# Expert rows packed in units of 64: 20 expert tiles a pass with four two-expert tiles, where there were 23 single-expert tiles

## The reference, cut to what matters

```python
B, T, D = 16, 512, 256
FF, E, TOPK = 1024, 8, 2
# for each of 1024 tokens, 2 experts are given (expert_indices, expert_weights)
hidden = gelu(layernorm(x_token) @ w1[e])      # 256 -> 1024
y      = hidden @ w2[e]                        # 1024 -> 256
x_out  = x_token + sum over its two experts of weight * y + bias
```

## Time and profile before

| | |
|---|---|
| median of three runs | 1342.62 us (1338.91 to 1346.79) |
| the profiled execution | 1340.46 us, its span 1338.7 us |
| TensorE busy | 1232.7 us, 92% of the span |
| VectorE / ScalarE / GpSimd busy | 67% / 54% / 45% |
| mean granted TensorE clock | 0.972 of 2.4 GHz |
| moved by DMA | 168.17 MB, 126 GB/s on average |

### The profile page before, as it was taken

How to read it: one execution, slowest core, us unless ns; L and a number is a source line. 1 busy time by engine, 2 the same in 40 slices (tenths; PEclk the granted TensorE clock), 3 DMA queues, 4 the chain that set the end, 5 groups by cost and what they waited for, 6 DMA issues and landing times. The chain is left out here.

```text
span 1338.7 us, 17191 instructions
## 1 busy us (share of the span) xinstructions
PE 1232.7 (92%) x6044; PEld 998.6 (75%) x6044; DVE 896.1 (67%) x1483; ACT 724.6 (54%) x1124; POOL 599.4 (45%) x534
## 2 busy tenths in 40 slices
PE   4699989999999999999988889899999999999982
PEld 2387677887878878888766658778778788888871
DVE  7998846557666665676878967578666665645354
ACT  3355443664735537356556657467666463553632
POOL 5335554346351442525747627367434522224014
PEclk9799999999999999999989979899999999999996
DMA  7001343647365472563230023665446644554554
GB/s 213 16 25 40 86 124 105 187 124 207 102 185 149 125 205 92 149 191 118 68 94 16 17 64 119 157 164 140 128 115 163 172 146 139 179 154 131 123 162 130
DMA packets 107333, 168.17 MB, mean 126 GB/s; under 512 B 10024, under 2 KB 85296, under 8 KB 107248
## 3 DMA queue, kind: packets, MB, share of 16 engines
q1 hardware_dynamic: 88016, 120.39, 28.1%
q0 software_dynamic: 12608, 40.65, 15.3%
q10 hardware_dynamic: 6624, 6.03, 1.3%
HBM read 134.79 MB, written 17.06 MB: 113 GB/s over the span
## 5 line engine op out<-in xcount | busy, mean ns | idle before, releaser
L1930 PE MATMUL psum<-fwv,hid 128*128 128x256 f32 x1024 | 239.6, 383 | 0.0
L576 POOL TENSOR_TENSOR rstd<-varis,half_neg 128x4 f32<-128x4 f32 x64 | 93.8, 1465 | 309.6 <-DVE varis L2721 145.4
L1930 PEld LDWEIGHTS psum<-fwv,hid 128*128 128x128 f32 x1024 | 193.6, 193 | 27.0 <-issue 1.0
L1971 PEld LDWEIGHTS psum<-xst,ew 128*128 128x128 f32 x1472 | 178.6, 193 | 17.1 <-issue 6.5
L1971 PE MATMUL psum<-xst,ew 128*128 128x128 f32 x1472 | 181.0, 276 | 5.6 <-ACT xst L1092 3.2
L1979 PE MATMUL psum<-ew,hidt 128*128 128x256 f32 x736 | 166.9, 380 | 2.7 <-ACT hidt L1098 2.7
L1979 PEld LDWEIGHTS psum<-ew,hidt 128*128 128x128 f32 x736 | 138.8, 190 | 24.8 <-ACT hidt L1098 3.5
L580 POOL TENSOR_SCALAR xhat<-rows_ring,negmean,rstd 128x256 f32<-128x256 f32 x108 | 110.9, 1039 | 18.7 <-PE psum L1840 12.3
L1098 ACT ACTIVATE hidt<-psum 128x512 f32<-128x512 f32 x92 | 54.9, 597 | 108.3 <-PE psum L1971 108.2
L1005 ACT ACTIVATE hid<-psum 128x512 f32<-128x512 f32 x128 | 74.7, 596 | 64.6 <-PE psum L1851 44.2
L693 POOL DMA_INDIRECT xs<-xf_rows,token_of_slot x46 | 56.3, 1224 | 88.5 <-PE psum L1959 74.2
(11 more groups left out here) (277 smaller groups left out, 2465.6 us busy)
## 6 DMA issues: line engine op xcount, KB each, us to landing
ew<-in_w SPq DMA_DIRECT2D x92, 1024.0 KB, 5.7
rows_ring<-bias_rows POOLq DMA_DIRECT2D x28, 512.0 KB, 5.6
rows_ring<-in_x SPq DMA_DIRECT2D x14, 512.0 KB, 4.6
rows_ring<-y POOLq DMA_DIRECT2D x14, 512.0 KB, 6.4
out<-rows_ring SPq DMA_DIRECT2D x14, 512.0 KB, 5.0
rows_ring<-space POOLq DMA_DIRECT2D x12, 512.0 KB, 4.7
ys_rows<-ys ACTq DMA_DIRECT2D x46, 128.0 KB, 4.8
xf_rows<-ew SPq DMA_DIRECT2D x2, 1024.0 KB, 4.6
```

Source lines behind the costliest of these rows:

```text
L576: pool.tensor_tensor(dst, src, half_neg[:, 0:src.shape[1]], ALU.pow).then_inc(done, 1)
L1930: last = nc.tensor.matmul(rows4[:, k, :], hid[:, j % NHID, k * P:(k + 1) * P], fwv[:, j, :], start=j == 0 and k % 2 == 0, stop=j == FC - 1 ...
L1971: last = nc.tensor.matmul(bank_e[:, j * P:(j + 1) * P], ew1[:, c, at:at + P], xst[:, c, :], start=c == 0, stop=c == DC - 1)
```

## The change

The rows of an expert are now counted in units of 64. A pass needs at most 2048/64 + 8 - 1 = 39 units, so 20 tiles (NT) of two units do. 16 of them are plain: both units are of one expert. Four, the mixed tiles, hold two units that may be of different experts (the odd unit that an expert has left over). The table of experts has 24 entries a pass, 16 for the plain tiles and 2 for each mixed one. The places "d" of turns 5 to 7, "x" of turns 14 and 15 and "d" of turn 16 are gone, so there are 40 tiles in all, and eight of them are mixed: those at "a" of turns 5, 6, 7, 8, 14 and 15, "d" of turn 11 (run at the start of turn 12) and "b" of turn 13.

A mixed tile turns its first product around: the 64 token columns of a unit are the weights and 512 columns of that unit's w1 move, so tokens come out on the partitions, unit 0 on partitions 0 to 63 and unit 1 on 64 to 127 (`two_up`). In the built program these matmuls have an array tile of 128x64 at column 0 or 64, where all of a plain tile's have 128x128. ScalarE copies the 128x512 result to `hid_rows` (`rows_of_two`), TensorE transposes it (`two_turn`), and the gelu follows as before. The second product has 64 columns of `hidt` as weights, once for each unit (`two_down`). A mixed tile needs two experts' w1 and w2, 4 MB through the same 2 MB buffer: the front half of the buffer takes the first halves of both w1, the back half the second halves, and each is overwritten by half of both w2 after `two_up(n, 0)` and `two_up(n, 1)`.

```diff
+UNIT = P // 2
+UNITS = NASG // UNIT + E - 1
+NT = (UNITS + 1) // 2
...
+MIXED_AT = ((5, "a"), (6, "a"), (7, "a"), (8, "a"), (11, "d"), (13, "b"), (14, "a"), (15, "a"))
...
             def load_expert(n):
...
-                e = sp.value_load(table[0:1, n % NT:n % NT + 1], min_val=0, max_val=E - 1)
-                if n:
+                experts = uses(n) if n in MIXED else [expert_in(tile_of(n))]
+                if n - 1 in MIXED:
+                    sp.wait_ge(half_down.sem, half_down.count(MIXED.index(n - 1), "h"))
+                elif n:
                     await_step(sp, up, n - 1, "b")
+                if n in MIXED:
+                    for x, e in enumerate(experts):
+                        load_w1(two_w1[0][:, x], e, slice(0, FF // 2))
+                else:
+                    load_w1(ew1, experts[0], slice(0, FF))
...
+            def load_mixed_w2(n):
+                experts = uses(n)
+                for half_no in range(2):
+                    await_step(sp, up, n, "ab"[half_no])
+                    for x, e in enumerate(experts):
+                        load_w2(two_w2[half_no][:, x], e, half_no * FC // 2, FC // 2)
...
+            def rows_of_two(n, half_no):
+                await_step(act, up, n, "ab"[half_no])
+                nc.scalar.activation(hid_rows[:], bank_e, ACT.Copy).then_inc(rows_up.sem, 1)
...
+            def two_up(n, half_no):
+                if half_no == 0:
+                    pe.wait_ge(xst_ready, n + 1)
+                else:
+                    await_step(pe, gelu, n, "a")
+                pe.wait_ge(slot_loaded[half_no], landed(n, 1))
+                for c in range(DC):
+                    for x in range(2):
+                        last = nc.tensor.matmul(bank_e[unit_rows(x), :], xst[:, c, unit_rows(x)], two_w1[half_no][:, x, c, :],
+                                                start=c == 0, stop=c == DC - 1)
+                last.then_inc(up.sem, 1)
+
+            def two_turn(n, half_no):
+                await_step(pe, rows_up, MIXED.index(n), "ab"[half_no])
+                for j in range(4):
+                    last = nc.tensor.transpose(bank_e[:, j * P:(j + 1) * P], hid_rows[:, j * P:(j + 1) * P], ident[:])
+                last.then_inc(turned.sem, 1)
+
+            def two_down(n):
+                await_step(pe, gelu, n, "b")
+                for half_no in range(2):
+                    pe.wait_ge(slot_loaded[half_no], landed(n, 2))
+                    for j in range(4 * half_no, 4 * half_no + 4):
+                        for x in range(2):
+                            last = nc.tensor.matmul(bank_e[unit_rows(x), 0:D], hidt[:, j, unit_rows(x)],
+                                                    two_w2[half_no][:, x, j % 4, :], start=j == 0, stop=j == FC - 1)
+                    if half_no == 0:
+                        last.then_inc(half_down.sem, 1)
+                last.then_inc(tiles_done, 1)
```

More of the change, by code:

```diff
@@ L72 @@
 TURN_OF = {n: i for (i, _), n in TILE_AT.items()}
+MIXED = [TILE_AT[at] for at in MIXED_AT]
+assert sum(n < NT for n in MIXED) == NMIX and len(MIXED) == 2 * NMIX
 NORM_TURN = [3, 10]
@@ L96, in await_step, with tile_of, landed @@
     eng.wait_ge(steps.sem, steps.count(min(run, steps.runs - 1), name))
+def tile_of(n):
+    before = sum(n - n % NT <= m < n for m in MIXED)
+    return PLAIN + before if n in MIXED else n % NT - before
+def landed(n, part):
+    return 16 * (n + 3 * sum(m < n for m in MIXED) + (2 * part if n in MIXED else 1))
 def numbered(name, n):
@@ L364, in hybrid_kernel @@
         last_pow = steps("last_pow", ["ln", "p"], 1)
-        route = steps("route", ["idx", "expert", "one", "rank", "n", "nf", "ni", "start", "end", "pos", "past", "tab",
-                                "slot"], 1)
+        route = steps("route", ["idx", "expert", "one", "rank", "n", "u", "p", "uf", "two", "left", "upto", "shift", "from", "at",
+                                "ends", "moved", "row", "pos", "past", "past2", "second", "late", "tab", "slot"], 1)
         route_pe = steps("route_pe", ["spread", "counts", "ends", "slots", "experts"], 1)
@@ L2186, in turn @@
                 p = only_rec(i)
-                a, b, c, d = (TILE_AT[i, place] for place in "abcd")
+                a, b, c = (TILE_AT[i, place] for place in "abc")
                 tile_in(a)
                 value_columns(i)
-                tile_up(a, 0)
+                two_up(a, 0)
                 recept_columns(i)
-                tile_up(a, 1)
+                two_turn(a, 0)
                 freed(ev2, i - 1, "e1")
@@ L2195, in turn @@
                 transposes_rec(p)
+                two_up(a, 1)
                 channel_key(i - 1, 0)
+                two_turn(a, 1)
                 channel_key(i - 1, 1)
-                tile_down(a)
                 freed(ev3, p, "c1")
                 receptances(i - 1)
+                two_down(a)
                 channel_key(i - 1, 2)
@@ L2408, in turn_12 @@
                 channel_key(11, 0)
-                tile_in(25)
+                tile_in(22)
                 channel_key(11, 1)
-                tile_up(25, 0)
+                two_up(22, 0)
                 channel_key(11, 2)
-                tile_up(25, 1)
+                two_turn(22, 0)
                 channel_key(11, 3)
+                two_up(22, 1)
                 freed(ev2, 11, "e1")
@@ L2562, in turn_15 @@
             def turn_15():
-                tile_in(37)
+                tile_in(33)
                 value_columns(15)
-                tile_up(37, 0)
+                two_up(33, 0)
                 channel_key(14, 0)
-                tile_up(37, 1)
+                two_turn(33, 0)
                 recept_columns(15)
+                two_up(33, 1)
                 channel_key(14, 1)
-                tile_down(37)
+                two_turn(33, 1)
                 freed(ev2, 14, "e1")
@@ L2573, in turn_15 @@
                 transposes_rec(13)
-                tile_in(38)
+                two_down(33)
                 channel_key(14, 2)
-                tile_up(38, 0)
                 channel_key(14, 3)
-                tile_up(38, 1)
                 channel_value(14, 0)
-                tile_down(38)
                 freed(ev3, 13, "c1")
```

571 lines of the change are left out of this document (307 added, 264 removed).

## The result

The changed kernel takes 1368.41 us in the median of four runs (1367.65 to 1370.07); the kernel before takes 1340.76 us beside it (1338.11 to 1346.79). The ratio is 1.0201, with a 95% interval of 1.0163 to 1.024: 27 us slower, where 13.5 us faster was forecast. The profiled execution has a span of 1366.0 us, against 1338.7.

A forecast was written before the change was run, and what follows sets the result against it. TensorE, busy 92% of the span, was taken as the bound. Terms -43.4 - 1.7 + 14.6 + 2.5 + 5.1 + 4.6 + 4.8 gave -13.5 us: 1329.1 us, 1.0% faster, range 1318 to 1375.

The forecast's parts named there:

- The side-by-side work: Mixed tiles on TensorE: two array halves overlap, half a `two_up` in 5 steps, `two_down` in 17; eight tiles 14.6 us dearer.
- The six tiles: Six tiles fewer on TensorE at 7.24 us each take out 43.4 us.
- The changes of the array's tile: Mixed tiles switch between 128x128 and 128x64, 48 changes at 0.05 us each, 2.5 us; bounds 0 and 0.14 a change.
- Rivals 1 and 2: Mixed tiles: columns take turns, 1371 us, chance 0.22; weight loads not hidden under the other column's matmul, 1351 us, chance 0.12.
- The middle norm: Turns 5 to 7: `rec_products` waits 1.7 us each for `norm_mid` to empty the transposes' banks, 5.1 us.
- The wait at the end (about 13 us): TensorE idles about 13 us before the last `rec_products`; of the last tile's 7.24 us, 4.8 are lost.
- Waits of 1.7, 1.7 and 1.2: 4.6 us: `two_down` waits for w2 in turns 14, 15 and 8, landing 6.2 us after issue; nothing in turns 5 to 7, 12, 13.
- the prediction's own sign of being wrong: Waits before the mixed tiles' steps adding up to more than 15 us would show the forecast wrong.
- Rival 3: Traffic of 4 MB around each mixed tile makes w2 or next w1 land late (11.8 us); 1346 us, chance 0.06.
- Nothing was put for the clock: The sum held no term for time lost to TensorE's half clock; forecast 0.
- "I put nothing" for ScalarE: ScalarE's 16 copies of 0.60 us for 12 gelus and 12 short copies fewer cost nothing, as it has room (54%).
- the removed tiles as pure gain: Removed tiles counted as -43.4 us of TensorE time, and -1.7 us of waits at the next turn's `tile_in`.

The follow-up runs named there:

- plain_40: The changed kernel with its eight mixed tiles run as plain tiles of one expert, the second expert's rows multiplied by wrong matrices; ratio 0.9904 to the kernel before.
- no_w2: The changed kernel without loading the mixed tiles' second matrices, their second product using what the first matrices left in the buffer; ratio 1.0003 to the kernel before.
- quiet: The changed kernel with POOL's two adds of the bias into rows_ring issued behind the gather for the next tile; ratio 1.0051 to the kernel before.
- fill_half: The changed kernel with 8, 8, 14 and 5 scratch matmuls ahead of the mixed tiles' second product in turns 6, 7, 14, 15; ratio 1.0162 to the kernel before.
- early_acts: The changed kernel with a relu earlier in turn 8, and conv_in and its transposes one step earlier in turn 12; ratio 1.0111 to the kernel before.
- x_outer: The changed kernel with all left-half matmuls issued before the right half's in both products of a mixed tile; ratio 1.0214 to the kernel before.

## Why the prediction was wrong

- **The side-by-side work: right that it happens, and the sum by luck near.** -26.3 us forecast, -28.8 measured, but no term was right by itself. The six tiles gave 41.4 us of work (plain_40), not 43.4. The mixed tiles cost 12.6, not 14.6 + 2.5 = 17.1, and this by two errors against each other. The overlap is better than forecast: both halves of the array start together, so half a `two_up` is four steps and not five, and `two_down` 16 and not 17; no right record waits for the second left one. The changes of the array's tile are dearer: about 0.3 us for a change and back, 0.15 a change, where 0.05 was taken and 0.14 was the upper bound: some 7 us instead of 2.5. The steps alone cost 6 us (2 x 1.72 + 3.46 + 0.87 for 7.02, eight times), and 6 + 7 is about the 12.6 that was measured.
- **What the rivals said of the array.** Rivals 1 and 2 are refuted, although the time fell within 3 us of rival 1's 1371: a total that fits a rival is no evidence for it, the group of L2055 is. The Trainium skill's rule that different column groups run concurrently ("TensorE: Matmul & The Clock Gate", Part 3) holds here, with 6.9/3.61 = 1.9x for two column tiles. Its rule of the same part that weights load beside matmuls only where the row group differs does not hold for this kernel's f32 records (the same part also names the background weight buffer, and the rows go with that). A drain when the tiling mode changes ("TensorEngine Tiling (Array Packing)", Key Properties, in the Trainium skill) would show as a cost like these 0.3 us; that it is a drain isn't shown, since nothing here changes the tile without changing the weights' columns too.
- **The middle norm: right** in its cause, with 3 x 1.54 = 4.6 us for 5.1. **The wait at the end (about 13 us): right**, 13.03, and the merges take 7.41 us unbroken as forecast (7.4). What was missed there is a second wait on the same chain, 5.25 us ahead of the gate products of p = 15, of which before shows 0.5.
- **"Waits of 1.7, 1.7 and 1.2: 4.6 us": the step that failed.** 16.3 us were measured: 3.9 in turn 6, 3.8 in turn 7, 6.4 in turn 14, 2.3 in turn 15, none in turn 8. (More than 15 us was the prediction's own sign of being wrong.) The term took the landing of 1 MB issued alone from the earlier trace rows, at its median, and put nothing for turns 5 to 7, where nearly 9 us of TensorE work stand between (406.88 to 415.7 in turn 6). But the DMA engines weren't free: 2 MB of second matrices, a gather, and two adds of 512 KB were under way together, and the landing took 12.3 us. Rival 3 had this mechanism, with 11.8 us from the same rows, in three turns and at 0.06; it was the likeliest place for the sum to break, since its row was the maximum of the earlier trace rows and the traffic around a mixed tile is greater than around any tile of before. no_w2 and quiet show it.
- **Nothing was put for the clock: 15.3 us.** The prediction took every wait at its own length. Seven of the new or longer waits were followed by a stretch at 1.2 GHz; no_w2 took 10.3 us of it away, fill_half 12.8.
- **"I put nothing" for ScalarE in turns 8 and 12, and the removed tiles as pure gain.** no_w2 leaves a miss of 18 us. plain_40, with 41 us less work, was 13 us faster. Two gelus and two copies per mixed tile stand in one in-order queue ahead of the relu that a `channel_key` waits for (3.5 us in turn 8, shown by early_acts), and removed tiles covered chains at the end (12.9 + 5.2 us in plain_40, for 7.22 + 0.5). Left open are the wait for VectorE in turn 13, 3.8 us with mixed tiles and 1.8 in plain_40, with its 1.7 us of half clock, and 1.8 us at the start of turn 8 that every kernel with 40 tiles has: no run isolates them.

## What to carry to other kernels

When work is taken from a busy engine, add to every wait that comes to light what the clock costs after it, and price a load by everything that the DMA engines carry between its issue and its need, not by the landing of a lone one. Before work is removed, look for what it covers: here 41 us less of it made the kernel only 13 to 20 us faster. A total that lands on a rival's number doesn't prove the rival, and a part sum that comes out right doesn't prove its terms.

## What the runs showed of the hardware that wasn't expected

- Two matmul streams on different 64-column halves of the array run side by side even when the program has up to four records of the other half ahead; with eight ahead, four ran alone (x_outer).
- Loads of the weights of one half don't hold up the other: 32 records of 256 columns took 3.61 us from start to start, 16 steps of 0.216 and 0.15 more.
- A change from the 128x128 array tile to 128x64 and back took about 0.3 us: 3.52 and 3.54 us for the eight-record groups ahead and behind, which take 3.44 elsewhere, and 0.15 inside.
- While the packets of two accumulating DMAs of 512 KB were at work (411.2 to 417.6 us in after) the DMA engines moved 240 GB/s and were fully busy; in quiet, without them and as busy (406 to 411 us), 355.
- After an idle time of 3.85 us TensorE worked on for 0.7 us at 2.4 GHz, and then for 3.4 us at 1.2; this made the wait cost about 5.6 us. A stretch at 1.2 GHz also followed a wait of 2.08 us in turn 12.
